# Inner layers of the gated network as seven block products in place of eight, two of the four token-block sums on GpSimd

## The reference, cut to what matters

```python
h = silu((xn @ w1.T) * w1_s) * ((xn @ w2.T) * w2_s)   # 256 -> 1024
h = gelu((h @ h1.T) * h1_s)                            # 1024 -> 1024
h = gelu((h @ h2.T) * h2_s)                            # 1024 -> 1024
y = (h @ w3.T) * w3_s                                  # 1024 -> 256
```

## Time and profile before

| what | value |
|---|---|
| median of three runs | 1150.59 us (1147.7 to 1152.03) |
| the profiled execution, its own time | 1144.51 us |
| its span, first to last instruction | 1142.7 us |
| mean granted TensorE clock | 0.984 |
| PE busy | 1074.3 us, 94% of the span |
| DVE, ACT, POOL busy | 563.0, 538.3, 193.8 us |

### The profile page before, as it was taken

How to read it: one execution, slowest core, us unless ns; L and a number is a source line. 1 busy time by engine, 2 the same in 40 slices (tenths; PEclk the granted TensorE clock), 3 DMA queues, 4 the chain that set the end, 5 groups by cost and what they waited for, 6 DMA issues and landing times. The chain is left out here.

```text
span 1142.7 us, 14257 instructions
## 1 busy us (share of the span) xinstructions
PE 1074.3 (94%) x5478; PEld 885.4 (77%) x5478; DVE 563.0 (49%) x850; ACT 538.3 (47%) x773; POOL 193.8 (17%) x185
## 2 busy tenths in 40 slices
PE   3579988999999999999999999999999999999997
PEld 3457877888767677888888778888888888888886
DVE  6585568654546647777875522332411411512412
ACT  3345776666634344655545543233443433533532
POOL 3144335331614232221120000000000000000000
PEclk9789999999999999999999999999999999999999
DMA  9767973544585545222310753301500100100100
GB/s 339 270 221 246 333 250 130 184 157 161 171 327 184 155 158 203 93 75 93 123 63 19 285 195 111 111 1 37 203 0 1 56 1 1 56 1 1 37 1 19
DMA packets 50502, 144.86 MB, mean 127 GB/s; under 512 B 4048, under 2 KB 16976, under 8 KB 49360
## 3 DMA queue, kind: packets, MB, share of 16 engines
q1 hardware_dynamic: 50432, 143.90, 36.3%
HBM read 102.99 MB, written 49.29 MB: 133 GB/s over the span
## 5 line engine op out<-in xcount | busy, mean ns | idle before, releaser
L1635 PE MATMUL pr<-b_hi,wh 128*128 128x512 f32 x512 | 201.7, 394 | 2.1 <-DMA wh<-w_s 2.1
L1635 PE MATMUL pr<-b_lo,wh 128*128 128x512 f32 x512 | 202.7, 396 | 0.0
L1094 ACT ACTIVATE full<-pr,prm 128x512 f32<-128x512 f32 x96 | 66.1, 689 | 228.4 <-PE pr L1635 172.2
L1486 DVE TENSOR_TENSOR a_lo<-full,a_hi 128x512 fp32r<-128x512 f32 x96 | 66.2, 690 | 182.6 <-ACT a_hi L1094 182.2
L1635 PEld LDWEIGHTS pr<-b_hi,wh 128*128 128x128 f32 x512 | 96.1, 188 | 25.0 <-DMA wh<-w_s 2.2
L1635 PEld LDWEIGHTS pr<-b_lo,wh 128*128 128x128 f32 x512 | 96.1, 188 | 23.4
L1635 PE MATMUL pr<-u_hi,ring 128*128 128x512 f32 x256 | 103.0, 403 | 2.3 <-issue 1.3
L1635 PE MATMUL pr<-a_hi,wh 128*128 128x512 f32 x256 | 101.9, 398 | 0.0
L1635 PE MATMUL pr<-a_lo,wh 128*128 128x512 f32 x256 | 101.5, 396 | 0.0
L1635 PE MATMUL pr<-u_lo,ring 128*128 128x512 f32 x256 | 100.6, 393 | 0.0
L704 POOL TENSOR_TENSOR xg_lo<-xg_lo,xg_hi 128x1024 fp32r<-128x1024 f32 x8 | 19.8, 2469 | 398.3 <-ACT xg_hi L899 398.3
(11 more groups left out here) (201 smaller groups left out, 2431.4 us busy)
## 6 DMA issues: line engine op xcount, KB each, us to landing
ring<-w_s SPq DMA_DIRECT2D x42, 512.0 KB, 4.9
wh<-w_s SPq DMA_DIRECT2D x18, 512.0 KB, 10.8
b_lo<-h_s SPq DMA_DIRECT2D x4, 2048.0 KB, 9.1
stage<-w_gated SPq DMA_DIRECT2D x4, 1536.0 KB, 10.1
ring<-w_s SPq DMA_DIRECT2D x2, 2560.0 KB, 11.1
vw<-v_s SPq DMA_DIRECT2D x8, 514.0 KB, 5.7
xt<-x SPq DMA_DIRECT2D x8, 512.0 KB, 7.3
xn_s<-xh SPq DMA_DIRECT2D x8, 512.0 KB, 7.8
```

The lines of the kernel that those rows point to most:

```text
L1094: last = e.activation(out_, hidden_banks[m % 4], ACT.Gelu, scale=par(scale, m))
L1486: e.tensor_tensor(out_lo[:, m, :], full2[:, m % 2, :], out_hi[:, m, :].bitcast(F32), ALU.subtract) \
L1635: return e.matmul(bank, w.bitcast(dt), v_.bitcast(dt), start=first, stop=last)
```

## The change

The inner layers of the last stage (12 of them; the four `h1` layers interleaved in the first stages stay) are computed by the Winograd form of Strassen's scheme. The 1024 x 1024 weight is cut in four blocks of 512 x 512, the activation in four blocks of 512 channels x 256 tokens, and seven products of blocks take the place of eight. Four sums of weight blocks (S1 to S4) are formed once for each layer by POOL in the second stage and kept in DRAM (`s_s`). Four sums of token blocks are formed for each layer and tile: T1 and T2 by DVE, T3 and T4 by POOL. DVE adds the products' results in five sums per layer and tile. Weights and moving blocks have one buffer per product, and the parts of the next tile are made while this one's products run.

```diff
+PRODUCTS = (("A11", "B11", 2, False), ("S1", "T1", 0, False), ("S2", "T2", 1, False), ("A12", "B21", 2, True),
+            ("S3", "T3", 1, False), ("S4", "B22", 0, False), ("A22", "T4", 1, True))
+HB = KH // 2
+HT = TOK // 2
+RESULTS = ((0, 0), (1, 1), (0, 1), (1, 0))
...
+LATE_SUMS = {(0, "last"): (0,), **{(i, "first"): (i,) for i in range(1, 8)}}
-LATE_CHECKS = {1: range(0, 2), 2: range(2, 4), 3: range(4, 5), 4: range(5, 7), 5: range(7, 9), 6: range(9, 10)}
+LATE_CHECKS = {1: (0, 1), **{i: (i,) for i in range(2, 8)}}
...
+            def late_sums(u):
...
+                pool.tensor_tensor(to[:, 0, :], a21, a22, ALU.add).then_inc(s["s_sum"], 1)
+                pool.tensor_tensor(to[:, 2, :], a11, a21, ALU.subtract).then_inc(s["s_sum"], 1)
+                pool.wait_ge(s["s_sum"], before + 1)
+                pool.tensor_tensor(to[:, 1, :], to[:, 0, :], a11, ALU.subtract).then_inc(s["s_sum"], 1)
+                pool.wait_ge(s["s_sum"], before + 3)
+                pool.tensor_tensor(to[:, 3, :], a12, to[:, 1, :], ALU.subtract).then_inc(s["s_sum"], 1)
...
             for i in E_STEPS:
                 if valid(i + 2):
                     halo(i + 2, x1, "g_x1", 1, "x1_halo")
...
+                for u in LATE_SUMS.get((i, "first"), ()):
+                    late_sums(u)
...
+            def combine(t):
+
+                inputs_in(pool, t, 2)
+                pool.wait_ge(s["u_lo"], X_BEFORE + NP * t + 2)
+                pool.wait_ge(s["x_f"], 4 * t + 2)
+                pool.tensor_tensor(tf[0][:], quarter(uf, 1, 1), quarter(uf, 0, 1), ALU.subtract).then_inc(s["x_f"], 1)
+                pool.wait_ge(s["u_lo"], X_BEFORE + NP * t + 3)
+                pool.wait_ge(s["x_f"], 4 * t + 3)
+                pool.tensor_tensor(tf[1][:], quarter(uf, 1, 0), tf[1][:], ALU.subtract).then_inc(s["x_f"], 1)
...
                 if valid(i + 3):
                     add_lepe(i + 3)
+                checks = [(u, n, what) for u in LATE_CHECKS.get(i, ()) for n, what in enumerate(checks_of(u))]
+                for late in checks[:3]:
+                    check_late(*late)
...
-                for n in LATE_CHECKS.get(i, ()):
-                    check_late(n)
+                for late in checks[3:]:
+                    check_late(*late)
...
+            for r in range(1, TILES):
+                t_, more = BLOCK_RUNS + r, r + 1 < TILES
+                scale_half(r - 1, 1)
+                if more:
+                    combine(t_ + 1, 1)
+                    low_part(t_ + 1, 0)
+                scale_half(r - 1, 0)
+                if more:
+                    low_part(t_ + 1, 1)
+                sums_to_u2(t_)
+                sums_to_u4(t_)
+                if more:
+                    combine(t_ + 1, 2)
+                result_22(t_)
+                low_of_result(r, 0)
+                if more:
+                    low_part(t_ + 1, 2)
+                result_12(t_)
+                if more:
+                    low_part(t_ + 1, 3)
+                low_of_result(r, 1)
+                low_of_result(r, 2)
+                result_21(t_)
+                if more:
+                    low_part(t_ + 1, 4)
+                    low_part(t_ + 1, 5)
+                low_of_result(r, 3)
+                if more:
+                    low_part(t_ + 1, 6)
...
+            def product(t, p, wide):
+                _, _, pair, more = PRODUCTS[p]
+                e.wait_ge(wb_in[p], wb_before[p] + 16 * (1 if t < BLOCK_RUNS else 2))
+                e.wait_ge(s["u_lo"], X_BEFORE + NP * t + p + 1)
...
+                if p == 3:
+                    e.wait_ge(s["p1_kept"], t + 1)
+
+                e.wait_ge(s["u_sum"], max((0, 5 * t - 1, 5 * t, 0, 5 * t + 1, 5 * t + 2, 5 * t + 3)[p], 0))
+                to = quarters(pr[pair])
+                for m in range(HB):
+                    for k in range(HB):
+                        for i, x_ in enumerate((xp_hi[p], xp_lo[p])):
+                            last = add(to[:, m, :], wb[p][:, m, k * P:(k + 1) * P], x_[:, k, :], wide,
+                                       not more and m % 2 == 0 and k == 0 and i == 0, k == HB - 1 and i == 1)
+                last.then_inc(s["prod"], 1)
...
             def gated_network(wide):
...
+                for t_ in range(BLOCK_RUNS):
+                    first_layer(FRONTED + t_, wide)
+                    for p in range(NP):
+                        product(t_, p, wide)
+                for r in range(TILES):
+                    product(BLOCK_RUNS + r, 0, wide)
+                    if r >= 1:
+                        down(r - 1, 3, wide)
+                    for p in range(1, NP):
+                        product(BLOCK_RUNS + r, p, wide)
+                    for k in range(3):
+                        down(r, k, wide)
+                down(TILES - 1, 3, wide)
```

More of the change, by code:

```diff
@@ L324, in program, with quarter @@
+        a_lo = [a_at[i] for i in (0, 1, 2, 0)]
+        results = (c11, p1s, u4, u2)
+        ot = place("ot", [P, SUB, C], wo_at)
+        def quarter(buf, half, tokens):
+            return buf[:, half * HB:(half + 1) * HB, tokens * HT:(tokens + 1) * HT]
+        sources = (quarter(uf, 0, 0), tf[0][:], tf[1][:], quarter(uf, 1, 0), tf[0][:], quarter(uf, 1, 1), tf[1][:])
         pr = [ctx.enter_context(nc.psum_tensor(f"pr{i}", [P, 2, TOK], F32)) for i in range(4)]
@@ new lines, in save_result, with load_h @@
+            def save_result(t, k):
+                half, tokens = RESULTS[k]
+                sp.wait_ge(s["c_gelu"], gelus(t, k))
+                sp.dma_start(quarter(h_s[FRONTED + t], half, tokens), results[k][:]).then_inc(s["h_saved"][k], 16)
+            def load_h(j, half):
+                last = BLOCK_RUNS + j - 1
+                if half == 0:
+                    sp.wait_ge(s["u_lo"], X_BEFORE + NP * last + 1)
+                    sp.wait_ge(s["x_f"], 4 * last + 3)
+                    for i in range(HOUT):
+                        sp.wait_ge(s["h_saved"][i], H_BEFORE + 16 * max(j + 1 - FRONTED, 0))
+                else:
+                    sp.wait_ge(s["u_lo"], X_BEFORE + NP * last + 6)
+                    sp.wait_ge(s["x_f"], 4 * last + 4)
+                part = slice(half * HB, (half + 1) * HB)
+                sp.dma_start(uf[:, part, :], h_s[j][:, part, :]).then_inc(s["h_in"][half], 16)
@@ L496, in start_second_half, with load_y, store @@
+            def load_y(j):
+                sp.wait_ge(s["out_sum"], 2 * j)
+                sp.dma_start(yg[:], y_s[j]).then_inc(s["y_in"], 16)
+            def store(j):
+                for half in (1, 0):
+                    sp.wait_ge(s["out_sum"], 2 * j + 2 - half)
+                    sp.dma_start(out[j][:, 2 * half:2 * half + 2, :], ot[:, 2 * half:2 * half + 2, :]) \
+                        .then_inc(s["out_stored"], 16)
             def start_second_half():
@@ new lines, in keep_first, with gelu_block @@
+            def keep_first(t):
+                e.wait_ge(s["prod"], NP * t + 1)
+                result_free(e, t, 1)
+                e.copy(p1s[:], quarters(pr[2])).then_inc(s["p1_kept"], 1)
+            def gelu_block(t, k):
+                if k == 0:
+                    e.wait_ge(s["prod"], NP * t + 4)
+                    result_free(e, t, 0)
+                else:
+                    e.wait_ge(s["u_sum"], 5 * t + 2 + k)
+                source = (quarters(pr[2]), p1s, u4, u2)[k]
+                scale = "h1_s" if t < BLOCK_RUNS else "h2_s"
+                for m in range(HB):
+                    last = e.activation(results[k][:, m, :], source[:, m, :], ACT.Gelu, scale=par(scale, RESULTS[k][0] * HB + m))
+                last.then_inc(s["c_gelu"], 1)
@@ new lines, in _ @@
+            sums_to_u2(BLOCK_RUNS)
+            sums_to_u4(BLOCK_RUNS)
+            low_part(BLOCK_RUNS, 5)
+            low_part(BLOCK_RUNS, 6)
+            result_22(BLOCK_RUNS)
+            low_of_result(0, 0)
+            result_12(BLOCK_RUNS)
+            low_of_result(0, 1)
+            low_of_result(0, 2)
+            result_21(BLOCK_RUNS)
+            combine(BLOCK_RUNS + 1, 1)
+            low_part(BLOCK_RUNS + 1, 0)
+            low_part(BLOCK_RUNS + 1, 1)
+            combine(BLOCK_RUNS + 1, 2)
```

594 lines of the change are left out of this document (396 added, 198 removed).

## The result

| kernel | median, us | ratio to the kernel before, 95% interval |
|---|---|---|
| before (4 runs) | 1149.2 | 1 |
| changed (4 runs) | 1136.03 (1130.81 to 1138.99) | 0.9878 [0.9835, 0.9921] |
| changed, a second time, label after_again (7 runs; before 1147.02) | 1135.46 (1130.92 to 1143.38) | 0.9915 [0.9884, 0.9946] |

The change makes the kernel about 1% faster, 12 to 13 us and not 30. The direction was right; 1136 lies 2 us outside the forecast range (1109 to 1134) and 15 us above the forecast (1121).

What follows compares the result with a forecast made beforehand. The prediction took PE's matmuls as the bound, with PE busy 94% of the span. Its terms, -39.0 - 0.7 - 1.2 + 8.0 + 3.0 = -29.9 us, took 1150.6 to 1121 us, range 1109 to 1134.

Steps and rivals of the forecast that it cites:

- Matmuls, -39.0: Last stage: 224 half-width matmuls replace 128 full-width ones, 3.25 us less in each of twelve inner layers, -39.0 us.
- not cheaper: Last stage: half-width matmuls cost 132.8 ns, saving nothing, about 1160 us, or 174 ns, about 1271; chance 0.05.
- DVE the bound: Last stage: POOL and long queues stretch DVE's 19 instructions a tile until they eat the gain; about 1221 at double; chance 0.04.
- Second stage, +8.0: Second stage: checks alternate with POOL's `gate` and `bias_residual`, so PE waits for `pe_lo` in four steps, +8.0 us.
- upper bound of 14.8: Second stage: late sums also hold up `low_of_gelu` and the taps, 1.7 us more in each of four steps.
- Start of the last stage, -0.7: Start of last stage: fewer weights come first, so PE waits only for `y_out(7)` and starts at about 656.6, -0.7 us.
- Last stage's waits, +3: Last stage: DVE, ACT, POOL and loads mostly keep up with the matmuls; +3 us, bounds 0 and 12.
- the second rival: Last stage: instruction lists come late at every layer, 1 to 2.5 us for each of 12, time 1130 to 1148; chance 0.17.
- the save of the last quarter: Last stage: `sums_to_u2` waits for this save, 2.2 us of room or 2.4 us of stall in three tiles.
- End, -1.2: End of kernel: two half-width DVE instructions remain after the last matmul in place of two 1024-wide ones, -1.2 us.

Runs made afterwards that it cites:

- checks_behind: Changed kernel with all late weight checks of a step moved behind `pm_lo`; 1138.36 us, ratio 0.9924.
- v1: Complete kernel: sums_prev plus checks one by one ahead of `low_of_gelu`, maximum of the bits and its matmul further ahead; 1123.1 us, ratio 0.9809.
- sums_prev: Changed kernel with GpSimd's sums for late weights moved to the end of the step before; 1128.04 us, ratio 0.9842.
- v2: v1 with the second half of `uf` loaded ahead of the store and the load of `y`; 1119.39 us, ratio 0.9761.
- v3: v2 with the checks placed in VectorE's gaps and the maximum of the bits behind `low_of_gelu(7, 3)`; 1117.22 us, ratio 0.9754.
- sums_memset: Changed kernel with GpSimd's four late sums per unit replaced by memsets, weight sums left out; 1126.16 us, ratio 0.9805.
- checks_tiny: both_off, with each late check reading only 8 of its 1024 columns; 1118.62 us, ratio 0.9776.
- before_ahead: Kernel before the change, with only its own checks moved ahead of `low_of_gated`; 1152.16 us, ratio 1.0065.
- both_off: Changed kernel with the edits of checks_behind and sums_memset together; 1127.8 us, ratio 0.9822.
- sums_on_dve: Changed kernel with T3 and T4 of each tile formed by DVE in POOL's place; 1135.23 us, ratio 0.9877.
- flag_early: Changed kernel without the last unit's checks, the flag's sum right behind `fc1(7, 7)`; 1134.44 us, ratio 0.9895.

## Why the prediction was wrong

- **Matmuls, -39.0: right.** The last stage went from 479.4 to 450.1 us (682.99 to 1133.1). With its 8.1 us of waits and the 2.8 of slow clock taken off that would be 40.2 saved; the steady stretch has 0.118 us a matmul and no wait. The rivals "not cheaper" and "DVE the bound" fall with it.
- **Second stage, +8.0: the step that failed, by its size.** The one wait that it priced came out: PE waited 2.5, 1.4, 1.4 and 2.5 us on `pe_lo` where 2.6, 1.4, 1.4 and 2.6 were worked out. But the stage grew by 19.7 us (18.9 in after_again), past the upper bound of 14.8 too. Four parts were missing from the 8.0: waits for gelu 3.0, the flag's sum 1.9, `pm_lo` 0.8, and 5.8 us more of PE's busy time, of which 3.4 are the lower clock behind the two waits of 2.50 us. The first I had named for the bound (the late sums "hold `low_of_gelu` and the taps up"), then set to nothing. `bits` I had not followed: the last unit's four checks are in step 7, with the flag behind them. The clock I had taken as given. And the experiments show that the cost isn't a sum of waits in places: checks_behind took away 7.7 us of one and got 10.5 more of another. What was to be weighed was all that DVE and POOL get to do in the stage, and beside what it stands, and not one gap. DVE's busy time went from 209 to 254 us. Of these 45 us the 16 further checks (26 for 10) are 19 at 1.21 us each; the rest is instructions drawn out beside POOL's, and v1, with the same checks and sums in another order, has 223 us.
- **Start of the last stage, -0.7: wrong.** It waits 3.05 us for 2.07, +1.0, and the clock takes up to 2.8 more at this place. Over the whole last stage changed and sums_prev differ by 1.2 us only, since sums_prev has a stretch of low clock of its own, behind a wait of 2.3 us at some 911 us, that costs 1.6. `y_out` was through at 681.21, so PE wasn't held by it, as I had said it would be: in v1, v2, v3, sums_prev and sums_memset it is. I had followed the loads of `wgu` and `xg2`, and not those of the weight sums, which can't be issued before the last late sum is stored; the gap goes with how early they go out (last section).
- **Last stage's waits, +3: too low.** 8.1, of which 6.9 around the first `h2` tiles and 1.2 at the end, none in a layer of the steady tiles; so not the second rival, which would have had them everywhere. I had looked at the save of the last quarter, in three tiles; the places were the second tile's low parts beside T3 and T4, and the load of `uf`, which I had given room until 22 of 34 us.
- **End, -1.2:** 4.1 us from the last matmul to the end for 6.0, -1.9.

With the measured terms in place of the four that were off: -39.0 + 3.8 - 1.9 + 19.7 + 8.1 = -9.3 us. From the first `pe_lo` to the end the two profiles differ by 10.5 (791.2 and 780.7), and after_again gives 11.1; the medians 13.2 and 11.6. Up to the first `pe_lo`, ahead of the work that the change moves, the profiled execution of the changed kernel lost 5.0 us and after_again none (351.49); over the 14 profiles this point lies between 348.6 and 356.6 us, so the 5.0 are scatter.

## What to carry to other kernels

When work moves to engines that are not the bound, cost it where it is put and then add it up over the stage: a list that is nearly full gives the delay back at the next wait, so removing one wait (checks_behind) can show nothing, and taking the work itself away (checks_tiny) shows its price. A better order takes part of that price away (v1: 9.2 of 19.7 us). Work on GpSimd beside VectorE instructions with two SBUF inputs costs both. One moved line (sums_prev) was worth 7.4 us, more than half of the 11.6 that the whole change brought beside it, and not only by the waits that it was moved for. An experiment that moves work can meet a second cause in its new place, as before_ahead met a late load: look at each wait before the total is put down to the first. Behind a wait of TensorE look at the granted clock as well as at the wait.

## What the runs showed of the hardware

**Both sides of the alternation pay.** Beside checks, POOL's `gate` and `bias_residual` took 3.3 us for 2.4, and its late sums 1.74 us for 1.29 beside `h_lo`, which took 1.05 for 0.69.

**The clock behind a wait.** Behind each of the two 2.50 us waits of the second stage some eight matmuls ran at the lower level, 1.7 us lost; after the 3.05 us wait 17 us were granted 0.82 on average. At the start of the last stage the 14 profiles fall in two groups: behind 1.6 to 2.2 us of idle time the first 5 us were granted 1.00 in all seven, behind 3.1 to 4.6 us 0.50 to 0.71 in all seven. Elsewhere shorter waits were enough: 1.9 us in v1 and 2.3 in sums_prev, both among the first `h2` tiles, while waits of 2.3 us in the changed kernel and in before_ahead had none behind them. So the length of the wait alone doesn't tell. In checks_tiny, with the 7.8 us of idle time in short pieces, PE's busy time is that of before.

**The gap at the start of the last stage goes with the DMA traffic in it.** Over 14 profiles: with 12 to 80 GB/s in the gap it was 1.6 to 2.2 us (v3, v1, sums_memset, sums_prev, v2), with 118 to 140 2.0 to 2.1 (before_ahead, before), with 173 to 200 3.1 (changed, checks_behind, after_again), with 298 to 330 3.8 to 4.6 (both_off, checks_tiny, sums_on_dve, flag_early). From 3.1 us up PE waits there for nothing that the profile shows, at the branch on the flag, and in each profile one instruction transfer of 16 KB lies in the 8 us before PE starts or beside it. That the code for the branch comes in behind the weights is my reading of it; no run changed the one without the other, so it stays open. The traffic is a mean over the gap itself, and further weights are issued as the gap begins, so a longer gap also has more of it.

What decides when the burst of weights falls there can be read. The loads of the weight sums (`wb<-s_s`) wait until the last late sum has landed in DRAM; in the changed kernel the queue stands 12.1 us for that, and issues them 6.8 us before the last fc2 ends:

```profile
SPq L443 <- DMA s_s<-late_sum: 12.1, 1, 12.1
...
673.14 0.92 SPq L619 DMA_DIRECT2D wb<-s_s  x2
```

Where they go out 18 to 22 us before that end, the gap is 1.7 to 2.2 us (v1, v2, v3, sums_prev, all with the late sums one step earlier); 8.3 us before it, 1.6 (sums_memset); 6.8 to 7.0, 3.1 (changed, checks_behind, after_again); 5.9 to 6.2, 3.8 to 4.1 (both_off, checks_tiny, sums_on_dve); 4.3, 4.6 (flag_early). So over the 12 profiles with the new last stage the gap goes with how early these loads go out, and one edit, sums_prev, moved both: a part of its gain is this one. Why PE waits while they are under way stays open, as said.
